# A fused attention and expert block: cross attention moved two batches ahead, and the own attention's side work placed by one table

## What is computed

```python
x = x + tanh(g_xattn) * cross_attention(layernorm(x), ctx, ctx)      # 16 heads of 16, no mask
z = layernorm(x)
h = z + attention(rmsnorm(z, g1), wq, wk, wv, wo)                    # own: rotary q and k, causal
y = h + moe(rmsnorm(h, g2), w_router, wg, wu, wd)                    # 8 experts, top 2, hidden width 704
x = x + tanh(g_ffn) * y
```

## Time and profile before

| | |
|---|---|
| median of 3 runs | 1713.26 us (1711.63 to 1713.75) |
| the profiled execution | 1707.33 us, span of its trace 1705.6 us |
| TensorE | busy 1482.6 us (87%) |
| VectorE | busy 976.2 us (57%) |
| GpSimd | busy 932.4 us (55%) |
| ScalarE | busy 807.1 us (47%) |
| first score product, last attention product | 41 us, 1115 us |
| second block begins, its first gate product | 1164 us, 1180 us |

### The profile page before, as it was taken

One profiled execution on the slowest core, in us unless ns is written; L12 is line 12 of the kernel. 1 busy time (PEld: TensorE's weight loads), 2 busy tenths in 40 slices (PEclk: granted clock), 3 DMA queues, 4 the chain that ended last, 5 costly groups with the idle time before them and its releaser, 6 DMA issues. The chain is left out here.

```text
span 1705.6 us, 33019 instructions
## 1 busy us (share of the span) xinstructions
PE 1482.6 (87%) x9936; PEld 936.1 (55%) x9936; DVE 976.2 (57%) x2345; ACT 807.1 (47%) x1845; POOL 932.4 (55%) x1153
## 2 busy tenths in 40 slices
PE   1966989999999989989989987942999999999997
PEld 0212344444444444444443443432999999999997
DVE  1826667677677677677677555522444444444443
ACT  0451755755755755755755753521333333333332
POOL 5276766678678678678678353221334334433443
PEclk9987999989989999999999988966999999999999
DMA  5545564556455555556455434116142443244211
GB/s 171 156 128 157 162 180 134 155 158 199 151 171 186 155 173 183 160 173 186 147 182 163 145 121 111 63 37 255 54 147 60 151 150 122 93 151 151 61 57 32
DMA packets 112509, 238.41 MB, mean 140 GB/s; under 512 B 20624, under 2 KB 74772, under 8 KB 110295
## 3 DMA queue, kind: packets, MB, share of 16 engines
q1 hardware_dynamic: 76198, 147.66, 28.4%
q0 software_dynamic: 22656, 78.48, 13.4%
q10 hardware_dynamic: 13488, 10.17, 2.2%
HBM read 144.14 MB, written 93.14 MB: 139 GB/s over the span
## 5 line engine op out<-in xcount | busy, mean ns | idle before, releaser
L811 DVE TENSOR_REDUCE neg<-max_ps 128x1 f32<-128x512 f32 (+3 forms) x1024 | 564.6, 585 | 297.9 <-PE max_ps L492 150.1
L680 ACT ACTIVATE probs<-key_ps 128x512 f32<-128x512 f32 (+3 forms) x1024 | 499.5, 520 | 348.8 <-PE key_ps L509 197.8
L489 PE MATMUL max_ps<-k_stack,q_stack 96*128 96x512 bf16 (+3 forms) x1024 | 365.4, 362 | 75.0 <-DVE neg L811 33.9
L506 PE MATMUL key_ps<-q_stack,k_stack 99*128 99x512 bf16 (+3 forms) x1024 | 356.1, 351 | 22.7 <-ACT probs L680 17.5
L489 PEld LDWEIGHTS max_ps<-k_stack,q_stack 96*128 96x128 bf16 x1024 | 102.2, 100 | 293.3 <-DVE neg L811 173.4
L506 PEld LDWEIGHTS key_ps<-q_stack,k_stack 99*128 99x128 bf16 x1024 | 101.6, 100 | 153.4 <-ACT probs L680 92.7
L1448 PE MATMUL y_ps<-weights,hidden_t 128*128 x1278 | 171.4, 290 | 4.8 <-issue 3.4
L1448 PEld LDWEIGHTS y_ps<-weights,hidden_t 128*128 128x128 f32 x1278 | 158.3, 194 | 6.7 <-issue 6.7
L1424 PE MATMUL gate_ps<-weights,rows_t 128*128 x852 | 156.2, 332 | 6.5 <-DMA weights<-w_split 5.3
L1348 DVE TENSOR_TENSOR hidden<-silu,up_ps 128x352 f32<-128x352 f32 x142 | 74.0, 521 | 137.4 <-PE up_ps L1424 137.4
L1424 PE MATMUL up_ps<-weights,rows_t 128*128 x852 | 148.4, 323 | 0.0
(11 more groups left out here) (182 smaller groups left out, 2115.8 us busy)
## 6 DMA issues: line engine op xcount, KB each, us to landing
w_split<-w_parts POOLq DMA_DIRECT2D x32, 704.0 KB
weights<-w_split SPq DMA_DIRECT2D x8, 2816.0 KB, 11.0
weights<-w_split SPq DMA_DIRECT2D x8, 1280.0 KB, 13.1
rows<-rows_in ACTq DMA_DIRECT2D x71, 129.0 KB
w_split<-w_parts POOLq DMA_DIRECT2D x16, 512.0 KB
kept_sb<-kept SPq DMA_DIRECT2D x16, 512.0 KB, 5.8
parts_cross_q<-parts_q SPq DMA_DIRECT2D x48, 128.0 KB
parts_cross_k<-parts_k SPq DMA_DIRECT2D x48, 128.0 KB
```

What stands on the lines that cost most here:

```text
L489: r = mm(ps[:, 0:keys], q_stack[g][0:KROWS, hd, qt * P:(qt + 1) * P], k_stack[g][0:KROWS, hd, 0:keys], start=True, stop=not own)
L506: r = mm(ps[:, q0:S], k_stack[g][0:KROWS + NEGROWS, hd, kt * P:(kt + 1) * P], q_stack[g][0:KROWS + NEGROWS, hd, q0:S], start=True, stop=no ...
L680: act.activation(probs[:, kt % 2, hd, q0:S], key_ps[j % 2][:, q0:S], ACT.Exp).then_inc(m["exp_done"], 1)
L811: v.tensor_reduce(neg[:, g % 2, hd, qt:qt + 1], max_ps[(n * 16 + j) % MAX_RING][:, 0:keys], op=ALU.max, axis=AX.X, negate=True).then_inc(m ...
```

## The change

All engines get one table of the whole run in place of item numbers within a step. `at(i, u)` is item `u` of step `i` counted through, and `stage(i, s)` a stage. Every kind of side work has its row for each batch. Besides:

- The units' order becomes cross 0, cross 1, cross 2, own 0, cross 3, own 1, ..., cross 7, own 5, own 6, own 7, without holes. The steps run from -1 to 7. Cross 1's values go into the tile of the own values, own 6's into that of the cross values.
- For a regular own batch hn1 and q stand in stages 4 and 5 of the step before, k in 6 and 7, v in stage 2 of its own step. x and context of batch `i+3` are prepared in stages 0 and 1 of step `i`. x1 is summed over the border of two steps, routing is spread over stages 6 and 7.
- VectorE reads q and k for the rotation from `aux` itself. The copies of ScalarE and `flat` for them are gone, the scale is multiplied into `wq` once. The rotation and split on GpSimd go by halves of 128x512, four pieces in stages 0, 1, 1 and 2. Stores have a semaphore for each half.
- GpSimd instead of ScalarE makes the rows of hn2, which has two buffers now, and the two halves of a scatter move from stage 0 to stages 4 and 6 of the same step.
- The weight pieces have a table of counts per stage. In the last but one step there are eleven.
- At the start x, identity and context are loaded first. The first four transposes go to four banks, VectorE splits one half of k and both of q, GpSimd the other, and batch 1's x is normalised before the first step.

```diff
+UNITS = [("cross", 0), ("cross", 1)] + [unit for b in range(B - 2) for unit in (("cross", b + 2), ("own", b))] + [("own", B - 2), ("own", B - 1)]
 class Step:
-        self.cross = i + 1 if has(1) else None
-        self.own = i if has(0) else None
-        self.past = i - 1 if has(-1) else None
-        self.ahead = i + 2 if has(2) else None
+    def half(self, n):
+        u = 2 * (self.i + 1) + n
+        return (*UNITS[u], u) if 0 <= u < len(UNITS) else None
     def max_of(self, s):
-        u = self.named("cross" if s < 4 else "own")
+        u = self.half(s // 4)
...
-PIECES_AT = ((0,), (1,), (2,), (3,), (4,), (5,), (6, 7), ())
-    for i in range(-2, B + 1):
+STEPS = range(-1, B)
...
+X_TURNS = {1: at(-1, 2, 6), 2: at(-1, 50, 54), 3: at(0, 44, 48), **{b: at(b - 3, 4, 8) for b in range(4, B)}}
+C_TURNS = {1: at(-1, 10, 14), 2: at(-1, 66, 70), 3: at(0, 52, 56), **{b: at(b - 3, 18, 22) for b in range(4, B)}}
+X1_SUMS = {b: at(b - 2, 112, 128) for b in BATCHES} | {0: at(-1, 112, 114), 1: at(0, 46, 48), LAST: at(LAST - 2, 112, 114)}
+HN1_TURNS = {b: at(b - 1, 72, 76) for b in REGULAR_OWN} | {0: at(0, 4, 8), LAST - 1: at(LAST - 2, 44, 48), LAST: at(LAST - 1, 4, 8)}
+Q_HALVES = {b: at(b - 1, 81, 87) for b in REGULAR_OWN} | {0: at(0, 12, 17), LAST - 1: at(LAST - 2, 72, 77), LAST: at(LAST - 1, 12, 17)}
+K_HALVES = {b: at(b - 1, 105, 116) for b in REGULAR_OWN} | {0: at(0, 22, 27), LAST - 1: at(LAST - 2, 82, 87), LAST: at(LAST - 1, 22, 27)}
+V_HALVES = {b: at(b, 33, 38) for b in BATCHES} | {LAST - 1: at(LAST - 2, 118, 123), LAST: at(LAST - 1, 33, 38)}
+ATT_TURNS = {b: at(b + 1, 52, 56) for b in BATCHES} | {LAST - 1: at(LAST - 1, 114, 118), LAST: at(LAST, 48, 52)}
+WO_HALVES = {b: at(b + 1, 60, 66) for b in BATCHES} | {LAST - 1: at(LAST - 1, 122, 128), LAST: at(LAST, 56, 61)}
+HN2_TURNS = {b: at(b + 1, 93, 97) for b in BATCHES} | {LAST - 2: at(LAST - 1, 90, 94), LAST - 1: at(LAST, 18, 22), LAST: at(LAST, 78, 82)}
+LOGITS = {b: at(b + 1, 101) for b in BATCHES} | {LAST - 2: at(LAST - 1, 98), LAST - 1: at(LAST, 27), LAST: at(LAST, 87)}
+CHOICES = {b: at(b + 1, 103, 105, 107) for b in BATCHES} | {LAST - 2: at(LAST - 1, 100, 102, 104), LAST - 1: at(LAST, 29, 31, 33),
+                                                          LAST: at(LAST, 89, 91, 93)}
+RANKS = {b: at(b + 1, 112) for b in BATCHES} | {LAST - 2: at(LAST - 1, 107), LAST - 1: at(LAST, 36), LAST: at(LAST, 96)}
...
+XN_STAGE = {b: stage(b - 1, 0) for b in BATCHES} | {0: stage(-1, 7), 1: stage(0, 3), LAST: stage(LAST - 2, 7)}
+ROTATE_STAGES = {b: (stage(b, 0), stage(b, 1), stage(b, 1), stage(b, 2)) for b in REGULAR_OWN} | \
+    {b: (stage(i, s), stage(i, s), stage(i, s + 1), stage(i, s + 1)) for b, i, s in ((0, 0, 1), (LAST - 1, LAST - 2, 5), (LAST, LAST - 1, 1))}
+SCATTER_STAGES = {b: (stage(b + 2, 4), stage(b + 2, 6)) for b in BATCHES} | \
+    {LAST - 4: (stage(LAST - 2, 4),) * 2, LAST - 3: (stage(LAST - 1, 3),) * 2, LAST - 2: (stage(LAST - 1, 7),) * 2,
+     LAST - 1: (stage(LAST, 3), stage(LAST, 4)), LAST: (stage(LAST, 7),) * 2}
+PIECES_IN_STEP = {-1: (0, 0, 1, 1, 1, 0, 1, 1), 0: (2, 0, 0, 0, 1, 2, 2, 2), LAST - 2: (0, 0, 2, 3, 1, 0, 0, 1),
+                  LAST - 1: (1, 0, 0, 1, 2, 2, 3, 2), LAST: (0,) * 8}
...
+                def rotation(o, b, c):
+                    aux_full(dve, o, b, c)
+                    over(dve, m["rope_used"], 4 * (b - 1) + k + 1)
+                    v.tensor_tensor(with_cos[o][:, c, :], aux[:, :], rope_sb[:, 0, :], ALU.mult).then_inc(m["rope_cos"], 1)
+                    v.stream_shuffle(out=turned[o][:, c, :], in_=aux[:, :], mask=swap).then_inc(m["aux_free"], 1)
...
+                def hn2_rows(b):
+                    for t in range(QT):
+                        r = g_.tensor_scalar(hn2[b % 2][:, t, 0:D], h[:, t, :], r_h[:, t:t + 1], 0.0, ALU.mult, ALU.add)
```

More of the change, by code:

```diff
@@ L105, in is_self, with value_tile @@
+STEPS = range(-1, B)
 def is_self(which):
     return which != "cross"
-PIECES_AT = ((0,), (1,), (2,), (3,), (4,), (5,), (6, 7), ())
-def splits_on_dve(step):
-    return step.i in (-2, LAST)
+def value_tile(which, b):
+    return "own" if (which, b) == ("cross", 1) or is_self(which) and b != LAST - 1 else "cross"
 def run_steps(eng, body):
-    for i in range(-2, B + 1):
+    for i in STEPS:
         body(Step(i))
-AUX_USES = (("hn1", "own", DC), ("q", "own", DC), ("k", "own", DC), ("v", "own", DC), ("att", "past", DC), ("wo", "past", DC),
-            ("x", "ahead", DC), ("c", "ahead", DC), ("hn2", "past", DC), ("lg", "past", 1), ("rank", "past", 1))
@@ L128, in aux_turns, with at, stage @@
-def aux_turns():
[L130 to L138, removed]
-AUX_TURN = aux_turns()
+def at(i, *units):
+    return tuple(128 * i + u for u in units)
+def stage(i, s):
+    return 8 * i + s
+BATCHES = range(B)
@@ new lines, in pieces_in, with times, due @@
+def pieces_in(st):
+    count = lambda n: PIECES_IN_STEP.get(n // 8, (0, 0, 0, 2, 2, 1, 1, 2))[n % 8]
+    done = sum(count(n) for n in range(stage(-1, 0), st))
+    return range(done, done + count(st))
+def times(table, width=1):
+    return {u + w: (b, c, w) for b, row in table.items() for c, u in enumerate(row) for w in range(width)}
+def due(table, unit):
+    rows = ((b, row if isinstance(row, tuple) else (row,)) for b, row in sorted(table.items()))
+    return [(b, c) for b, row in rows for c, st in enumerate(row) if st == unit]
@@ new lines, in aux_turns, with parts_order @@
+def aux_turns():
+    named = (("x", X_TURNS), ("c", C_TURNS), ("hn1", HN1_TURNS), ("q", Q_HALVES), ("k", K_HALVES), ("v", V_HALVES),
+             ("att", ATT_TURNS), ("wo", WO_HALVES), ("hn2", HN2_TURNS), ("lg", LOGITS), ("rank", RANKS))
+    begun = sorted((u, (name, b, c)) for name, table in named for b, row in table.items() for c, u in enumerate(row))
+    assert len({u for u, _ in begun}) == len(begun)
+    return {use: n for n, (_, use) in enumerate(begun)}
+AUX_TURN = aux_turns()
+def parts_order(ahead, name):
+    o = (0, 2)["qk".index(name)]
+    fills = [(ahead[b], "x" if name == "q" else "c", b) for b in ahead] + [(ROTATE_STAGES[b][o], "oq" if name == "q" else "ok", b) for b in BATCHES]
+    return [(kind, b) for _, kind, b in sorted(fills)]
@@ L364, in load_stack @@
                     hs = slice(g * HG, (g + 1) * HG)
[L365 to L367 removed]
+                    for o, sent in (("q", "oq" if kind == "own" else "x"), ("k", "ok" if kind == "own" else "c")):
+                        if g % 2 == 0 and o in sides:
+                            over(sp, m[f"{sent}_st{g // 2}"], (b + 1) * 48)
@@ L642, in body @@
                 def body(step):
-                    body_start(step)
                     for s in range(8):
```

1039 lines of the change are left out of this document (572 added, 467 removed).

## The result

| | before | after |
|---|---|---|
| median of 5 runs each, on one chip | 1713.26 us (1703.86 to 1715.65) | 1700.58 us (1697.67 to 1704.2) |
| ratio | | 0.9924, 95% interval 0.9904 to 0.9944 |
| span of the profiled execution | 1705.6 | 1698.8 |
| first score product, last exponential of attention | 41.0, 1114.1 | 28.5, 1103.4 |
| that stretch, TensorE busy in it | 1074, 964.7 | 1075, 963.6 |

The change gains 0.8%, not the 5% that were forecast. The page of the kernel after, to be held against the earlier trace rows: GpSimd has 36 us more, ScalarE 25 less, TensorE the same.

What follows compares the result with a forecast made beforehand. TensorE was taken to set the pace of attention's middle steps and starve at both ends; an earlier start, regular steps of 123 us and closed gaps ended attention at 1025, giving 1618 profiled, 1624 median, range 1590 to 1668.

Steps and rivals of the forecast that it cites:

- start: Before attention: reordered loads, fills and half-batch splits bring the first score product to 27.0 us, 14.0 earlier than 40.96.
- step -1: First attention step: two stages at VectorE's pace, 20 us, then six cross stages with some small waits, 82; 102 together.
- step 6 and the last stages: Attention's end: own-with-own step of 128.5 us including GpSimd 13 us late, then two last main stages of 25.5.
- What a stage costs: Attention stages: bare costs of 11.6 to 13.2 us plus 0.85 per piece of side work sum to a 122.0 us regular step.
- what goes is the wait in the seventh stage: Regular step: five items instead of two before the rank remove TensorE's wait; 123 us in place of 126.6.
- The clock: Regular step: 1 us added for TensorE at half speed, 0 if the clock never falls, 3.4 at most.
- the cover that I trust least: Regular step: GpSimd up to 7 us behind a stage's end, its maxima split needed about 7 us after; just holds.
- rival 2: Regular steps: GpSimd sets the pace, a step stays at 127 to 130 us, total around 1657; chance 0.15.
- rival 5: Own units' single-buffered stack: last k half late, TensorE waits once per step, slower at 1715 to 1740 us; chance 0.03.
- rival 4: Cross unit ahead does nothing: late stack loads, gaps of 27 and 19 us stay, total about 1680; chance 0.03.
- The rotation: VectorE's rotation products: reading PSUM directly takes near 680 ns instead of 988 ns for k; rotation costs nothing extra.
- The clock rule: Own stages: transposes don't count as busy like matmuls, so the clock stays slow more often; total 1672 us, chance 0.06.

Runs made afterwards that it cites:

- g3: Changed kernel with GpSimd instead of VectorE splitting both halves of the first queries, regular steps not edited: ratio 0.9946 to the kernel before.
- h2: Changed kernel, hn1 rows later, region-start sum out of the eighth stage, k rotation cut to 32 columns, GpSimd operations of 32 weight pieces left out: 0.9855.
- h4: h2 and besides, in batches 1 to 5, only the second of each projection's two products kept: ratio 0.9688 to the kernel before.
- e3: Changed kernel with six of the eleven weight pieces of step 6 moved to step 7: ratio 0.9853 to the kernel before.
- f4: e4 and besides a second buffer for the parts of a weight piece: ratio 0.9743 to the kernel before.
- f1: Changed kernel with the two GpSimd operations of each of 32 weight pieces in steps 1 to 4 left out: ratio 0.9894 to the kernel before.
- f2: Kernel before with the GpSimd operations of the same 32 weight pieces as in f1 left out: ratio 1.0026 to the kernel before.
- e4: Changed kernel with batch 1's context load earlier, hn1 rows at item 40, and six weight pieces moved from step 6 to 7: ratio 0.9799.
- g1: Changed kernel with routing positions and weights of batches 0 to 3 moved from the eighth stage to the next step's fourth: ratio 1.0021.
- h3: e4 with f4's second buffer and the routing count kept with the region start added, computing everything: ratio 0.9732 to the kernel before.

## Why the prediction was wrong

Forecast were 1618 for the profiled execution and 1624 for the median; measured were 1700.6 in both, outside both ranges (1605 to 1645, and 1590 to 1668). The direction was right. The 82 us, by the prediction's own steps (lengths from first reduction to first reduction):

| step of the sum | predicted | measured | off |
|---|---|---|---|
| start | 27.0 | 29.1 | +2 |
| step -1 | 102 | 116.2 | +14 |
| step 0 | 125 | 130.7 | +6 |
| step 1 | 123 | 138.7 | +16 |
| steps 2 to 4 | 369 | 388.6 | +20 |
| step 5 | 125 | 136.5 | +11 |
| step 6 and the last stages | 154 | 163.6 | +10 |
| behind it | 593 | 597.2 | +4 |

- **The start** was right: its first product stands at 28.51, within the bounds of 25 to 31. It is all that the changed kernel gains: the attention behind it is 1 us longer and what follows 4 us. Which of its parts carries it was not separated, only that it is not VectorE's splitting (g3).
- **The step that failed is "What a stage costs"**, and with it "what goes is the wait in the seventh stage". The bare prices were taken from one or two rows of stages with little or no side work, in steps with little else, and the sum was worked out for the new step alone: 122. It was not asked what it gives for the old one: the same pieces, so about 122 too, against 126.6 measured. The difference was put down to one wait of 4 us. The runs show what it is: over steps 2 to 4 TensorE idled 8.5 us a step before, 10.6 after, and 10.4 and 10.5 in h2 and h4; no edit of the changed kernel brought it under 10. With its 118 to 119 us busy a step of 123 would have needed idle time of 4 to 5. What makes up this idle time is a row of small waits for VectorE and ScalarE that change their names from run to run; why they don't shrink stays open. In place of 16.6 the seventh stage takes 18.8 with TensorE busy 17.4, and in place of 14.4 the eighth takes 17.4, held by VectorE.
- **The clock** was taken as 1 us. Two stages of the step shown stand at 0.89 and 0.90, about 3.5 us at 1.2 GHz in each. That costs 3.4 in the step, the upper end that was named, and as much as before (both kernels have 0.97 over the three steps). That is 2.4 of the 6.5 us by which a regular step is too long.
- **GpSimd.** "Up to 7 us behind", "it just holds" and "the cover that I trust least" was the right place with the wrong sign. In steps 1 and 5 it does not hold (9.3 us, and 2.84 and 2.14), and e3 and f4, which only help GpSimd, bring 0.7% and 0.6%. In step 6 its lateness was counted at 13 and measured at 9.16 + 6.70 = 15.9. As the setter of the regular pace (rival 2) it is refuted by f1. Rival 2's step of 127 to 130 us holds the measured 129.5, for a reason that the runs do not bear out; its 1657 misses by 44. The nearest totals on offer were rival 5's 1715 to 1740 and rival 4's 1680, and neither's mechanism came: the result lies between rivals.
- **Step -1**: 7.31 for the context load. TensorE was at 1.2 GHz from 38.4, in the midst of that wait, to 62.3 us, and again for part of the eighth stage, which took 18.6 at a granted clock of 0.72. The loads' order on the SyncE queue was in the diff, and "some small waits" stood for it.
- **The rotation** came out as predicted in its number: products of 680 ns. But 988 was read wrongly as the price of two operands in SBUF. It was k's mean alone; q's products took 685 from the same kind of operands. k's stood beside GpSimd's split and ended 0.54 us behind its operation, as in f2 with its 2.21. So reading `aux` saves 0.6 us in each batch and one exposure to GpSimd, and what moving the products out of the second stage was worth was not separated.
- **The clock rule** weighed in the prediction: in the step shown the own stages run at 1.00 but for the eighth (0.90), so the row was the better guide.

## What to carry to other kernels

Before a sum of stage costs prices the new kernel, let it price the old one; what it misses there belongs into the new sum as well, until an experiment has taken it away (here 8.5 us of idle TensorE a step became 10.6, and no edit brought it back under 10). Where stages have different engines near their limit, relief of one may come back in the next stage, and a stage that looks too long may be the cover of a queue in the next. Give every group of runs a control whose steps are not edited, as g3 was by luck: step lengths from another chip or another execution differ by as much as the edits. What did pay were waits of 5 us and more outside the steady state: clearly, side work taken out of a step that already had too much (e3), and just clear of the intervals, a second buffer behind a store (f4). A load's place in its queue and the later rows paid only together (e4 against e3).

## What was not expected of the hardware

Some short VectorE operations whose operands all lie in SBUF stood still while a GpSimd operation ran: 0.17 to 0.22 us became 1.25 to 1.90, with the end 30 to 50 ns behind GpSimd's in each of the rows shown, and 2.17 in g1, with the end 20 ns behind. A reciprocal of 4 columns did not (0.18 at 795.88, beside 795.79 to 796.40). One that reads `aux`, a PSUM bank, did not, in the midst of a GpSimd operation (0.18 at 787.27, beside 786.77 to 787.55). Small routing operations of a batch take 7.9 us after, 5.9 before. The Trainium skill states the cause (SBUF — State Buffer, section "SBUF: two separate sides"): the two engines share a pair of ports, and of a GpSimd operation and a VectorE operation with two inputs in SBUF or in a two-port mode the one that starts first holds it for the whole instruction, while the other waits. The trace agrees in the ends, to 0.05 us. In the starts it does not always: by the profile the cast started 0.60 us before the GpSimd operation that it ended with, and the one in g1 0.03 before. Reading the region starts into the count, so that only a PSUM operand is left (h3), does away with one of these operations.
